# Two hand-ordered programs for the first two bodies of a pipelined attention, mixture-of-experts and cross-attention kernel

## The chip, the cores and the metric

The kernel runs on one core of one Trainium2 chip. A core has TensorE for matrix products (PE in the profile), VectorE (DVE), ScalarE (ACT), GpSimd (POOL) and SyncE (SP), which here only issues DMAs. Each engine runs its own list of instructions in order, and engines wait for each other on semaphores. The metric is the device time of one execution in microseconds, the median over the runs.

## The reference, cut to what matters

x has 2 batches of 1024 tokens of width 256; the context has 64 keys of width 192 for each batch. Four sublayers follow one another, each on the layer norm of the running x:

```python
x = x + L0_xattn(layernorm(x), ctx)   # 16 heads of 16, then relu(out @ W1 + b1) @ W2 + b2 (width 512)
x = x + L0_ffn(layernorm(x))          # 1024-wide FFN, 8 experts of LoRA rank 16, top 2, gate = top-2 softmax sum
x = x + L1_xattn(layernorm(x), ctx)   # one head of width 256
x = x + L1_ffn(layernorm(x))          # x @ weight.T + pooled(x) @ disha
```

## The kernel before, in words

**Tiling.** The 2048 tokens are cut into 8 blocks of T = 256 (two tiles of 128). A block goes through three stages: A is the first sublayer, F the expert layer, C the last two sublayers. They are pipelined: `body(a, f, c, h)` does stage A of block a, F of block f = a - 1, C of block c = a - 2, and the norm and queries (the head of stage A) of block h = a + 1. Body 0 so has no F and no C part, and body 1 no C part. After body 7 come `drain` and `end`.

**Precision.** Most products run in three passes: a value is split into a high part, rounded to the fp32r type by ScalarE, and a low part, the difference, made by VectorE or GpSimd; the passes are high by high, low by high, high by low (`passes` L306, `three` L296). So each operand needs two elementwise steps before its last pass. Products of type F32 (constants, transposes, fillers, `a_attend`) leave two records each in the profile.

**Stage A.** `transposes(1, b)` (L322) turns the normed block; `a_queries` (L334) makes the queries in bank P_(0); ScalarE's `queries` (L798) and VectorE's `queries_low` (L1060) split them; SyncE's `stack_q` (L227) lays them out head by head in the tensor `stack` with 12 DMAs for a block, 8 that wait for the high part and 4 for the low part. `a_row_scores` (L345) and `row_max` give each query's maximum, which `a_max_transposes` and ScalarE's `maxima` (L804) put into `stack` too. Then come `a_scores` d = 0 to 3 (L367) into banks S_(0) and S_(1) in turn, ScalarE's `exps` (L811) behind each, `a_attend` m = 0, 1 (L383) into P_(0) and P_(1), VectorE's `attended` (L1071: a reciprocal and a product), the split of the result, `a_hidden` u = 0, 1 (L397, with W1), `a_out` (L408, with W2) and the residual with the statistics of the second norm.

**Stage F.** `f_gate` (L420), VectorE's `experts` (L1084: the top two and the masked LoRA rows), `f_lora_transposes` (L431), `lora_high` and `lora_low` (L1122); then for u = 0 to 3 `f_base` (L437, weights wi), `f_first` and `f_second` (both through L458), and `f_out` (L474, weights wo), all in banks I_(0) and I_(1). Stage C begins with `c_turn` (L490) at the end of the body before, ScalarE's `high(3, ...)`, VectorE's `low(3, ...)` and `c_scores` (L503).

**Work of the first bodies alone.** The weights are loaded once by SyncE and ScalarE and split by `high_weights` (ScalarE L880) and `low_weights` (VectorE L1351, GpSimd L1518). `constant_row`, `keys1`, `values1`, `folded_keys` (L570 to L603) and the three `fold_` functions (L528 to L553) fold the weights and the context of stage C together. `filler` (L618) multiplies zeros into a bank that nothing reads: 3 of them stand ahead of body 0 and 10 in it.

**What sets the order.** Every engine has the order written out by hand. All bodies share one function for each engine, with branches for the stages that a body has and for a == 0 and f == 0. SyncE's order is fixed too: all weights and the stacks of block 0, then for each block `stack_q(b, 0)`, `stack_q(b, 2)`, `stack_q(b, 1)` and the load of the next x.

Of the kernel before, what the change touches and what calls it, by code (L numbers as in the profile page):

```python
# [11 lines left out]
P = 128  # L12
# [6 lines left out]
T = 256  # L19
# [40 lines left out]
def build(nc, io):  # L60
# [135 lines left out]
    bvrow1, wq1t = (views(passing, PASSING)[n] for n, _ in PASSING)  # L196
    kt0_h, kt0_l = temp("kt0_h", [P, KC * P], F32R), temp("kt0_l", [P, KC * P], F32R)
    kd_h, kd_l = temp("kd_h", [P, BATCH * KC * P], F32R), temp("kd_l", [P, BATCH * KC * P], F32R)
    kt1 = temp("kt1", [P, KC * P])
# [18 lines left out]
    with block:  # L218
# [74 lines left out]
        def _(pe):  # L293
# [40 lines left out]
            def a_queries(b):  # L334
                if b == 0:
                    pe.wait_ge(S("lo_w"), 1)
                else:
                    pe.wait_ge(S("o32"), (b - 1) * KC + 1)
                parts = [(P_(0)[:, m * T:(m + 1) * T], w("wq", m * P), x_of(XTA)) for m in range(KC)]
                pe.wait_ge(S("ln1_h"), b + 1)  # L340
                passes(parts, range(KC), ((0, 0), (1, 0)), True, False)
                pe.wait_ge(S("ln1_l"), b + 1)
                passes(parts, range(KC), ((0, 1),), False, True).then_inc(S("q_ps"), 1)

            def a_row_scores(b, t, bank=S_):  # L345

                if t == 0:
# [35 lines left out]
            def a_attend(b, m):  # L383
# [5 lines left out]
                for d in (2 * m, 2 * m + 1):  # L389
                    pe.wait_ge(S("ex"), b * DPAIRS + d + 1)  # L390
                    for c in (2 * d, 2 * d + 1):
                        rows = slice(PW * (c % GPC), PW * (c % GPC) + PW)
                        mm(P_(m)[rows, 0:T], v0[:, at + c * PW:at + (c + 1) * PW], EX[:, c, :], start=True, stop=True)  # L393
                        last = mm(P_(m)[rows, T:2 * T], ones_pair, EX[:, c, :], start=True, stop=True)  # L394
                last.then_inc(S("pv"), 1)

            def a_hidden(b, u):  # L397
                if u == 0:
                    if b == 0:
                        pe.wait_ge(S("lo_w"), 2)  # L400
                    pe.wait_ge(S("oh"), (b + 1) * KC)
                parts = [(S_(u)[:, k * T:(k + 1) * T], w("w1", (2 * u + k) * P), x_of(OA)) for k in range(2)]
                passes(parts, range(KC), ((0, 0), (1, 0)), True, False)
                if u == 0:
                    pe.wait_ge(S("ol"), (b + 1) * KC)
                passes(parts, range(KC), ((0, 1),), False, True).then_inc(S("hs_ps"), 1)
# [121 lines left out]
            def fold_turn():  # L528
                pe.wait_ge(S("g_in"), BATCH)
# [128 lines left out]

            def body(a, f, c, h):
                A_, F_, C_, H_ = (v is not None for v in (a, f, c, h))  # L660
                if A_:
                    a_scores(a, 0)
                    a_scores(a, 1)
                if F_:
                    f_lora_transposes(f)
                if C_:
                    c_scores(c, 0)
                    c_scores(c, 1)
                if F_:
                    f_first(f, 0)  # L670
                    f_first(f, 1)
                if A_:
                    a_scores(a, 2)
                if a == 0:
# [943 lines left out]
```

## Time and profile before

| | us |
|---|---|
| median of 3 runs | 330.58 |
| lowest, highest | 329.61, 331.83 |
| the profiled execution, whole | 332.24 |
| its span, first to last instruction | 330.1 |
| mean granted TensorE clock in the span | 0.988 of full |

The trace is of the profiled execution, and its times count from the start of the span. A busy share is of the span. A matmul's record begins when it starts and ends at a modelled end, so records of neighbours overlap; the chain of waits gives each step only the time by which it moved the chain on. Body 0 begins with `a_scores(0, 0)`, body 1 at 52.25 us and body 2 at 89.41 us.

### The profile page before, as it was taken

What the parts mean: (1) busy time and instruction counts of PE and PEld (TensorE: products, weight loads), DVE (VectorE), ACT (ScalarE), POOL (GpSimd) and SP (SyncE); (2) the same over time, 40 slices, a digit from 0 to 9 for tenths busy, and PEclk for the clock granted to TensorE, in tenths of its full rate; (3) what the DMA queues carried; (4) which work ended last, traced back from release to release, by engine and by line L of the source; (5) the groups of instructions that cost most, each with busy time, mean ns of one, the idle gap of its engine ahead of it and who ended that gap; (6) DMA issues with size and microseconds to landing.
All of it is one profiled execution on the core that took longest, in us unless ns stands there. A gap on an engine that the chain in (4) does not pass through costs nothing.

```text
span 330.1 us, 6479 instructions
## 1 busy us (share of the span) xinstructions
PE 314.6 (95%) x2497; PEld 285.6 (87%) x2497; DVE 231.2 (70%) x644; ACT 173.7 (53%) x355; POOL 146.2 (44%) x150
## 2 busy tenths in 40 slices
PE   7989998999999999999999999999999999999982
PEld 5748897899988999899989997999899988999771
DVE  4746676747878667956886687677786669456766
ACT  3346746572585456564667267635854564534411
POOL 2563681636053723654173607280537234613341
PEclk9989999999999999999999999999999999999997
DMA  8589720003100230013000410032002200000000
GB/s 244 156 247 359 165 82 0 2 9 89 32 3 2 57 92 13 2 26 104 36 0 10 96 57 0 2 85 77 2 0 50 69 13 1 2 0 34 0 34 32
DMA packets 14702, 18.85 MB, mean 57 GB/s; under 512 B 2224, under 2 KB 11312, under 8 KB 14416
## 3 DMA queue, kind: packets, MB, share of 16 engines
q1 hardware_dynamic: 12640, 14.99, 16.9%
q10 hardware_dynamic: 2032, 3.44, 3.0%
q8 instruction: 20, 0.33, 0.4%
q14 instruction: 10, 0.08, 0.1%
HBM read 9.51 MB, written 2.62 MB: 37 GB/s over the span
## 4 chain that ended last, share of the span: by engine, by line
PE 76%; POOL 8%; ACT 5%; DVE 5%; DMA 2%; SPq 2%; issue 1%; DVEq 0%; POOLq 0%; ACTq 0%
PE psI L302 13%; PE psI L458 12%; PE psI L311 9%; PE psP L311 7%; PE psS L311 7%; PE psT L302 4%; POOL hid_l L1447 4%; PE psP L393 3%; POOL hs_l L1441 3%; PE psS L379 2%; PE psT L326 2%; PE psP L394 2%; PE psT L525 2%; ACT qu_h L801 2%; PE psI L620 1%; ACT hs_h L829 1%
## 5 line engine op out<-in xcount | busy, mean ns | idle before, releaser
L1428 POOL TENSOR_TENSOR rs<-ve,mhalf 128x2 f32<-128x2 f32 x30 | 22.3, 745 | 95.3 <-DVE ve L1053 95.3
L1447 POOL TENSOR_TENSOR hid_l<-r,hid_h 128x512 fp32r<-128x512 f32 x32 | 40.8, 1288 | 15.3 <-ACT hid_h L849 15.3
L1132 DVE SCALAR_TENSOR_TENSOR r<-psI,nbi,r 128x256 f32<-128x256 f32 x60 | 25.8, 479 | 25.3 <-PE psI L458 25.2
L458 PE MATMUL psI<-at_h,lb_h 128*128 128x256 f32 x120 | 36.5, 304 | 2.1 <-DVE at_l L1124 1.5
L1441 POOL TENSOR_TENSOR hs_l<-hs,hs_h 128x512 fp32r<-128x512 f32 x16 | 20.8, 1301 | 35.6 <-ACT hs_h L829 35.4
L458 PE MATMUL psI<-at_l,lb_h 128*128 128x256 f32 x120 | 33.9, 282 | 0.0
L458 PE MATMUL psI<-at_h,lb_l 128*128 128x256 f32 x120 | 33.8, 282 | 0.0
L1073 DVE RECIPROCAL rec<-psP 128x256 f32<-128x256 f32 x16 | 28.1, 1753 | 6.5 <-PE psP L394 6.5
L844 ACT ACTIVATE r<-psI,first 128x256 f32<-128x256 f32 x60 | 24.2, 469 | 13.6 <-PE psI L458 13.5
L458 PEld LDWEIGHTS psI<-at_h,lb_h 128*128 128x128 f32 x120 | 22.6, 188 | 8.7 <-issue 5.0
L813 ACT ACTIVATE ex<-psS 128x512 f32<-128x512 f32 x32 | 19.0, 596 | 20.2 <-PE psS L379 20.1
L791 ACT ACTIVATE xn<-xmid,nmr,rs 128x256 f32<-128x256 f32 x16 | 8.8, 598 | 37.1 <-POOL nmr L1432 37.1
L302 PE MATMUL psI<-xtf_h,wi_h 128*128 128x256 f32 x120 | 25.3, 292 | 0.0
L302 PE MATMUL psI<-xtf_h,wi_l 128*128 128x256 f32 x120 | 24.0, 281 | 0.0
L302 PE MATMUL psI<-xtf_l,wi_h 128*128 128x256 f32 x120 | 24.0, 281 | 0.0
L849 ACT ACTIVATE hid_h<-r 128x512 fp32r<-128x512 f32 x32 | 19.5, 628 | 7.7 <-DVE r L1132 7.4
L458 PEld LDWEIGHTS psI<-at_h,lb_l 128*128 128x128 f32 x120 | 22.7, 189 | 0.2
L458 PEld LDWEIGHTS psI<-at_l,lb_h 128*128 128x128 f32 x120 | 22.6, 189 | 0.0
L1069 DVE TENSOR_REDUCE mx<-psS 128x16 f32<-128x1024 f32 x15 | 18.3, 1221 | 5.4 <-PE psS L356 5.4
L1436 POOL TENSOR_TENSOR oa_l<-o,oa_h 128x256 fp32r<-128x256 f32 x16 | 11.8, 737 | 18.7 <-ACT oa_h L818 18.7
L807 ACT ACTIVATE stack<-psP 16x1024 fp32r<-16x1024 f32 x16 | 16.2, 1016 | 7.0 <-PE psP L365 6.8
L302 PEld LDWEIGHTS psI<-xtf_h,wi_h 128*128 128x128 f32 x120 | 18.3, 189 | 0.7
(258 smaller groups left out, 870.6 us busy)
## 6 DMA issues: line engine op xcount, KB each, us to landing
stack<-qu_h SPq DMA_DIRECT2D x60, 64.0 KB, 2.0
xin<-in_x SPq DMA_DIRECT2D x8, 256.0 KB, 2.8
stack<-qu_l SPq DMA_DIRECT2D x30, 64.0 KB, 2.0
out<-x ACTq DMA_DIRECT2D x7, 256.0 KB, 2.0
raw_wi<-in_wi SPq DMA_DIRECT2D x1, 1024.0 KB, 9.1
raw_wo<-in_wo SPq DMA_DIRECT2D x1, 1024.0 KB, 12.4
kv<-in_kv SPq DMA_DIRECT2D x2, 384.0 KB, 8.4
raw_w<-in_w ACTq DMA_DIRECT2D x1, 512.0 KB, 7.5
```

Source lines behind the costliest of these rows:

```text
L302: last = mm(out, lhs(a, c), rhs(b, c), start=start and q == 0 and k == 0, stop=stop and q == 2 and k == n - 1, **kw)
L311: last = mm(out, lhs(a, c), rhs(b, c), start=start and (a, b) == pairs[0] and i == 0 and k == 0, stop=stop and k == len(chunks) - 1, skip_ ...
L458: last = mm(bank[:, k * T:(k + 1) * T], (WH, WL)[x]["lb"][:, 0, f * P:(f + 1) * P], AT[y][:, which, :], start=False, stop=q == 2, skip_gro ...
L813: A(EX[:, 2 * d:2 * d + 2, :], S_(d % 2).rearrange("p (k n) -> p k n", k=2), ACT.Exp, scale=SCALE).then_inc(S("ex"), 1)
L844: last = A(R1[:, f, :], bank[:, k * T:(k + 1) * T], ACT.Relu, bias=cols[:, BI + f:BI + f + 1])
L849: A(HH[:, 2 * u:2 * u + 2, :], R1[:, 2 * u:2 * u + 2, :], ACT.Identity).then_inc(S("hidh"), 1)
L1069: V.reduce_max(MX[:, t, :], ps[:, :].rearrange("p (h k) -> p h k", h=HEADS), AX.X).then_inc(S("mx"), 1)
L1073: V.reciprocal(REC[:, m, :], P_(m)[:, T:2 * T]).then_inc(S("rec"), 1)
L1132: last = V.scalar_tensor_tensor(out=R1[:, f, :], in0=bank[:, k * T:(k + 1) * T], scalar=nbi[:, f:f + 1], in1=R1[:, f, :], op0=MAX, op1=ADD)
L1428: G_.tensor_tensor(rs[:, :], ve[:, :], mhalf[:, :], ALU.pow).then_inc(S(f"ln{j}_rs"), 1)
L1441: G_.tensor_tensor(HS[1][:, two, :], HS32[:, two, :], as32(HS[0][:, two, :]), ALU.subtract).then_inc(S("hsl"), 1)
L1447: G_.tensor_tensor(HL[:, two, :], R1[:, two, :], as32(HH[:, two, :]), ALU.subtract).then_inc(S("hidl"), 1)
```

## The change

The first two bodies get functions of their own, `first_body` and `second_body`, on TensorE, ScalarE, VectorE and GpSimd; the shared `body` runs from body 2 on and loses its branches, its order being the same. SyncE's list is unchanged.

- Ahead of body 0 the fillers go from 3 to 5; in it they go from 10 to 4 (in T_(0)).
- In the first body all four `a_scores` of block 0 stand first, then both `a_attend`. `a_queries(1)` and `a_hidden(0, 0)` are cut into a high and a low part that alternate. `a_hidden(0, u)` writes the banks I_(u) of the feed-forward part, which leaves S_ free: the first `a_row_scores` of block 1 go to S_(0) and S_(1), the second to T_(0) and T_(1), without waits for the hidden layer or for the first maximum, and the transposed maxima to S_(0).
- All of block 1's `a_scores` and `a_attend` move from the second body into the first; `a_attend(1, 0)` writes T_(0). `f_lora_transposes(0)` moves ahead of them and of `f_base(0, 1)`. `values1` goes to T_(1) and moves behind `a_attend(1, 0)`.
- The fold work moves: `folded_keys` and `fold_turn` from the first body into the second, and `fold_means` and `fold_values` to its later half. Their helpers on ScalarE (`folded_in`, v1t, vv_h, gw_h) and on VectorE (`values_bias`, wc_sum, gw, gw_l, vv_l) move along. `gw_l` now stands between `experts(1)` and `low(3, 0)`; before, it stood ahead of `hidden_sum(0, 3)`.
- ScalarE converts `wi` directly ahead of `hidden(0, 0)`, as before; `w2` moves between the two halves of `attended`, and `queries(1)` between `hidden_high(0, 0)` and `hidden(0, 1)`.
- The buffer kt1 gets another place; `a_attend` takes a bank as an argument like `attended` below.

```diff
-    def a_queries(b):
-        if b == 0:
-            pe.wait_ge(S("lo_w"), 1)
-        else:
-            pe.wait_ge(S("o32"), (b - 1) * KC + 1)
+    def a_queries(b, high=True, low=True):
         parts = [(P_(0)[:, m * T:(m + 1) * T], w("wq", m * P), x_of(XTA)) for m in range(KC)]
-        pe.wait_ge(S("ln1_h"), b + 1)
-        passes(parts, range(KC), ((0, 0), (1, 0)), True, False)
-        pe.wait_ge(S("ln1_l"), b + 1)
-        passes(parts, range(KC), ((0, 1),), False, True).then_inc(S("q_ps"), 1)
+        if high:
+            if b == 0:
+                pe.wait_ge(S("lo_w"), 1)
+            else:
+                pe.wait_ge(S("o32"), (b - 1) * KC + 1)
+            pe.wait_ge(S("ln1_h"), b + 1)
+            passes(parts, range(KC), ((0, 0), (1, 0)), True, False)
+        if low:
+            pe.wait_ge(S("ln1_l"), b + 1)
+            passes(parts, range(KC), ((0, 1),), False, True).then_inc(S("q_ps"), 1)
...
-            if b > 0:
+            if b > 1:
                 pe.wait_ge(S("hs"), b * NDH)
-        elif b > 0:
+        elif b > 1:
             pe.wait_ge(S("mx"), b * NT + t)
...
-    def a_max_transposes(b):
+    def a_max_transposes(b, bank=P_(1)):
...
-        if b > 0:
+        if b > 1:
...
-        nc.tensor.transpose(P_(1)[0:NT * MXW, 0:P], mx[:, :], ident).then_inc(S("mxT_ps"), 1)
+        nc.tensor.transpose(bank[0:NT * MXW, 0:P], mx[:, :], ident).then_inc(S("mxT_ps"), 1)
...
-    def a_hidden(b, u):
-        if u == 0:
-            if b == 0:
-                pe.wait_ge(S("lo_w"), 2)
...
+    def a_hidden(b, u, banks=S_, high=True, low=True):
+        parts = [(banks(u)[:, k * T:(k + 1) * T], w("w1", (2 * u + k) * P), x_of(OA)) for k in range(2)]
+        if high:
+            if u == 0:
+                if b == 0:
+                    pe.wait_ge(S("lo_w"), 2)
+                pe.wait_ge(S("oh"), (b + 1) * KC)
+            passes(parts, range(KC), ((0, 0), (1, 0)), True, False)
+        if low:
+            if u == 0:
+                pe.wait_ge(S("ol"), (b + 1) * KC)
+            passes(parts, range(KC), ((0, 1),), False, True).then_inc(S("hs_ps"), 1)
...
     def fold_turn():
-        pe.wait_ge(S("g_in"), BATCH)
         pe.wait_ge(S("v1"), 1)
...
     def values1():
         for b in range(BATCH):
-            last = values(I_(1)[:, b * D:(b + 1) * D], kv1[:, WV1:WV1 + 2 * D], b)
+            last = values(T_(1)[:, b * D:(b + 1) * D], kv1[:, WV1:WV1 + 2 * D], b)
         last.then_inc(S("v1_ps"), 1)
...
     def folded_keys():
         pe.wait_ge(S("kt1"), 1)
-        pe.wait_ge(S("crow"), 1)
         pe.wait_ge(S("ld_passing"), 32)
...
-        last.then_inc(S("g_ps"), 1)
         for k in range(KC):
-            last = mm(I_(0)[:, 0:P], cols[:, BQ1 + k:BQ1 + k + 1].broadcast_to([P, P]),
+            last = mm(T_(0)[:, KC * P:(KC + 1) * P], cols[:, BQ1 + k:BQ1 + k + 1].broadcast_to([P, P]),
                       kt1[:, k * P:(k + 1) * P], start=k == 0, stop=k == 1)
         last.then_inc(S("gb_ps"), 1)
...
+    def first_body():
+        for d in range(DPAIRS):
+            a_scores(0, d)
+        a_attend(0, 0)
+        a_attend(0, 1)
+        pe.wait_ge(S("v0"), BATCH)
+        filler(T_(0), 2)
+        transposes(1, 1, T_(1))
+        filler(T_(0), 2)
+        a_queries(1, low=False)
+        a_hidden(0, 0, I_, low=False)
+        a_queries(1, high=False)
+        a_hidden(0, 0, I_, high=False)
+        a_hidden(0, 1, I_)
+        a_out(0, 0)
+        pe.wait_ge(S("ex"), DPAIRS)
+        a_row_scores(1, 0)
+        a_row_scores(1, 1, T_)
+        a_out(0, 1)
+        a_max_transposes(1, S_(0))
+        constant_row()
+        keys1()
+        transposes(2, 0, T_(1))
+        a_scores(1, 0)
+        a_scores(1, 1)
+        f_gate(0, 1)
+        a_scores(1, 2)
+        a_scores(1, 3)
+        pe.wait_ge(S("crow"), 1)
+        a_attend(1, 0, T_(0))
+        values1()
+        pe.wait_ge(S("kt1"), 1)
+        f_base(0, 0)
+        f_lora_transposes(0)
+        pe.wait_ge(S("x1"), 1)
+        a_attend(1, 1)
+        f_base(0, 1)
+
+    def second_body():
+        f_first(0, 0)
+        f_first(0, 1)
+        pe.wait_ge(S("o32"), KC + 1)
+        folded_keys()
+        f_second(0, 0)
+        f_second(0, 1)
+        a_hidden(1, 0)
+        pe.wait_ge(S("v1"), 1)
+        transposes(1, 2, T_(1))
+        f_base(0, 2)
+        a_hidden(1, 1)
+        f_first(0, 2)
+        f_base(0, 3)
+        a_queries(2)
+        f_second(0, 2)
+        f_first(0, 3)
+        a_out(1, 0)
+        a_row_scores(2, 0)
+        a_out(1, 1)
+        f_second(0, 3)
+        pe.wait_ge(S("g_in"), BATCH + 1)
+        fold_turn()
+        fold_means()
+        f_out(0, 0)
+        a_row_scores(2, 1)
+        f_out(0, 1, low=False)
+        fold_values()
+        pe.wait_ge(S("gw"), 1)
+        transposes(2, 1, T_(1))
+        f_out(0, 1, high=False)
+        a_max_transposes(2)
+        f_gate(1, 2)
+        pe.wait_ge(S("vv_l"), 2)
+        c_turn(0)
+        f_base(1, 0)
+        f_base(1, 1)
...
-    filler(I_(0), 3)
-    for i in range(NBLK):
-        body(i, i - 1 if i >= 1 else None, i - 2 if i >= 2 else None, i + 1 if i + 1 < NBLK else None)
+    filler(I_(0), 5)
+    first_body()
+    second_body()
+    for i in range(2, NBLK):
+        body(i, i - 1, i - 2, i + 1 if i + 1 < NBLK else None)
     drain(NBLK - 1, NBLK - 2)
     end(NBLK - 1)
...
+    def folded_in():
+        act.wait_ge(S("gb_ps"), 1)
+        for b in range(BATCH):
+            A(GWR[:, :, b * (KEYS + D):b * (KEYS + D) + KEYS],
+              T_(0)[:, 0:KC * P].rearrange("p (c b k) -> p c b k", c=KC, b=BATCH)[:, :, b, :],
+              ACT.Identity).then_inc(S("g_in"), 1)
+        A(gb[:, :], T_(0)[:, KC * P:(KC + 1) * P], ACT.Identity).then_inc(S("g_in"), 1)
...

+    def first_body():
+        for d in range(DPAIRS):
+            exps(0, d)
+        normalise(1, 1, XIN)
+        high(1, 1, XTA, T_(1))
+        attended(0, 0)
+        high_weights("w2")
+        attended(0, 1)
+        high_weights("wi")
+        hidden(0, 0, I_)
+        hidden_high(0, 0)
+        queries(1)
+        hidden(0, 1, I_)
+        hidden_high(0, 1)
+        high_weights("ga")
+        high_weights("lb")
+        maxima(1, S_(0))
+        high_weights("wo")
+        normalise(2, 0, XMID)
+        high(2, 0, XTF, T_(1))
+        for d in range(DPAIRS):
+            exps(1, d)
+        sorted_exps(0)
+
+    def second_body():
+        lora_high(0)
+        act.wait_ge(S("v1"), 1)
+        A(VV[0][:, 0:2 * BATCH:2, :], r3(v1, BATCH), ACT.Identity).then_inc(S("vv_h"), 1)
+        first_relu(0, 0)
+        attended(1, 0)
+        first_relu(0, 1)
+        folded_in()
+        attended(1, 1)
+        normalise(1, 2, XIN)
+        sum_high(0, 0)
+        hidden(1, 0)
+        hidden_high(1, 0)
+        high(1, 2, XTA, T_(1))
+        sum_high(0, 1)
+        first_relu(0, 2)
+        hidden(1, 1)
+        queries(2)
+        hidden_high(1, 1)
+        first_relu(0, 3)
+        act.wait_ge(S("v1t_ps"), 1)
+        A(v1t[:, :], T_(0), ACT.Identity).then_inc(S("v1t"), 1)
+        sum_high(0, 2)
+        sum_high(0, 3)
+        act.wait_ge(S("gw"), 1)
+        A(gw_h[:, :], gw[:, :], ACT.Identity).then_inc(S("gw_h"), 1)
+        normalise(2, 1, XMID)
+        act.wait_ge(S("vw_ps"), 1)
+        A(VV[0][:, 1:2 * BATCH:2, :], T_(0).rearrange("p (b n) -> p b n", b=BATCH), ACT.Identity).then_inc(
+            S("vv_h"), 1)
+        high(2, 1, XTF, T_(1))
+        maxima(2)
+        high(3, 0, XTC, T_(0))
...
-    def attended(b, m):
+    def attended(b, m, bank=None):
+        bank = P_(m) if bank is None else bank
         dve.wait_ge(S("pv"), b * KC + m + 1)
-        V.reciprocal(REC[:, m, :], P_(m)[:, T:2 * T]).then_inc(S("rec"), 1)
+        V.reciprocal(REC[:, m, :], bank[:, T:2 * T]).then_inc(S("rec"), 1)
         dve.wait_ge(S("rec"), b * KC + m + 1)
-        V.tensor_tensor(O32[:, m, :], P_(m)[:, 0:T], REC[:, m, :], MULT).then_inc(S("o32"), 1)
+        V.tensor_tensor(O32[:, m, :], bank[:, 0:T], REC[:, m, :], MULT).then_inc(S("o32"), 1)
...
+    def first_body():
+        dve.wait_ge(S("x_in"), 2 * 16)
+        norm_stats(1, 1, XIN)
+        attended(0, 0)
+        attended(0, 1)
+        low(1, 1, XTA, T_(1))
+        low_weights("wi", 1, 2)
+        queries_low(1)
+        row_max(1, 0)
+        row_max(1, 1, psT)
+        first_residual(0)
+        dve.wait_ge(S("x1"), 1)
+        norm_stats(2, 0, XMID)
+        low_weights("ga")
+        low_weights("lb")
+        constant()
+        low(2, 0, XTF, T_(1))
+        experts(0)
+        gates(0)
+
+    def second_body():
+        values_bias()
+        lora_low(0)
+        attended(1, 0, T_(0))
+        attended(1, 1)
+        dve.wait_ge(S("x_in"), 3 * 16)
+        norm_stats(1, 2, XIN)
+        hidden_sum(0, 0)
+        hidden_sum(0, 1)
+        dve.wait_ge(S("vv_h"), 1)
+        V.tensor_tensor(VV[1][:, 0:2 * BATCH:2, :], r3(v1, BATCH), as32(VV[0][:, 0:2 * BATCH:2, :]),
+                        SUB).then_inc(S("vv_l"), 1)
+        low(1, 2, XTA, T_(1))
+        dve.wait_ge(S("ld_wc"), 16)
+        V.tensor_tensor(GWR[:, :, KEYS:KEYS + D], GWR[:, :, KEYS:KEYS + D],
+                        late[:, D:2 * D].unsqueeze(1).broadcast_to([P, KC, D]), ADD).then_inc(S("wc_sum"), 1)
+        hidden_sum(0, 2)
+        queries_low(2)
+        row_max(2, 0)
+        hidden_sum(0, 3)
+        first_residual(1)
+        dve.wait_ge(S("x1"), 2)
+        norm_stats(2, 1, XMID)
+        dve.wait_ge(S("gw_mean"), 1)
+        V.tensor_tensor(GWR, GWR, T_(1)[:, 0:GW].unsqueeze(1).broadcast_to([P, KC, GW]), SUB).then_inc(
+            S("gw"), 1)
+        row_max(2, 1)
+        low(2, 1, XTF, T_(1))
+        dve.wait_ge(S("vv_h"), 2)
+        V.tensor_tensor(VV[1][:, 1:2 * BATCH:2, :], T_(0).rearrange("p (b n) -> p b n", b=BATCH),
+                        as32(VV[0][:, 1:2 * BATCH:2, :]), SUB).then_inc(S("vv_l"), 1)
+        second_residual(0)
+        dve.wait_ge(S("x2"), NT)
+        statistics(3, 0, X2)
+        experts(1)
+        dve.wait_ge(S("gw_h"), 1)
+        V.tensor_tensor(gw_l[:, :], gw[:, :], as32(gw_h[:, :]), SUB).then_inc(S("gw_l"), 1)
+        low(3, 0, XTC, T_(0))
+        moments(3, 0)
...
+
+    def values_bias():
         dve.wait_ge(S("ld_passing"), 32)
         dve.wait_ge(S("v1_ps"), 1)
-        V.tensor_tensor(r3(v1, BATCH), I_(1).rearrange("p (b n) -> p b n", b=BATCH),
+        V.tensor_tensor(r3(v1, BATCH), T_(1).rearrange("p (b n) -> p b n", b=BATCH),
                         bvrow1.unsqueeze(1).broadcast_to([P, BATCH, D]), ADD).then_inc(S("v1"), 1)
...
+    def first_body():
+        scale(1, 1)
+        attended_low(0, 0)
+        attended_low(0, 1)
+        low_weights("w2", 0, 1)
+        hidden_low(0, 0)
+        hidden_low(0, 1)
+        low_weights("wi", 0, 2)
+        scale(2, 0)
+        residual(1)
+        pool.wait_ge(S("crow_ps"), 1)
+        low_weights("wo", 0, 2)
+        low_weights("wo", 1, 2)
+
+    def second_body():
+        pool.wait_ge(S("crow"), 1)
+        gated(0)
+        attended_low(1, 0)
+        attended_low(1, 1)
+        scale(1, 2)
+        sum_low(0, 0)
+        sum_low(0, 1)
+        hidden_low(1, 0)
+        hidden_low(1, 1)
+        sum_low(0, 2)
+        sum_low(0, 3)
+        scale(2, 1)
+        residual(2)
+        scale(3, 0)
+
```

## Rows read from the trace of the kernel before

**Rows 1.** The page: span, TensorE's busy share, its granted clock in 40 slices.
```profile
span 330.1 us, 6479 instructions
PE 314.6 (95%) x2497; PEld 285.6 (87%) x2497; DVE 231.2 (70%) x644; ACT 173.7 (53%) x355; POOL 146.2 (44%) x150
PEclk9989999999999999999999999999999999999997
```

**Rows 2.** Waits of TensorE: for whom, us in total, times, longest.
```profile
PE psI L458 <- DVE at_l L1124: 1.5, 1, 1.5
...
PE psS L379 <- DMA stack<-qu_l: 1.2, 1, 1.2
```

**Rows 3.** The chain of waits from 0 to 110 us: start, us, what.
```profile
22.62 1.03 PE psP L393 x8
...
28.89 2.16 PE psI L620 x10
31.05 2.85 PE psS L311 x24
...
39.85 3.45 PE psT L574 x16
43.30 0.89 PE psI L582 x8
44.20 1.73 PE psI L567 x8
...
46.36 0.89 PE psT L597 x8
...
52.88 0.45 PE psP L434 x4
...
54.83 1.67 PE psI L458 x12
...
56.73 0.59 PE psP L393 x8
...
90.48 1.76 PE psT L302 x12
```

**Rows 4.** Stretches of half a us: length, busy by engine, granted clock, DMA.
```profile
18.50:19.00 0.50, 0.01 (x1) 0.00 (x0) 0.39 (x1) 0.39 (x1) 0.50 (x1) 1.00 0.49 103
...
22.00:22.50 0.50, 0.50 (x2) 0.00 (x0) 0.00 (x0) 0.00 (x0) 0.46 (x1) 0.50 1.31 436
```

**Rows 5.** Timeline from 15 to 50 us, all engines: start, us, what.
```profile
20.23 0.42 SPq L246 DMA_DIRECT2D raw_wi<-in_wi  x1
...
24.60 1.76 DVE L1073 RECIPROCAL rec<-psP 128x256 f32<-128x256 f32 x1 [2.65 <-PE psP L394]
...
31.02 1.91 ACT L882 ACTIVATE wi_h<-raw_wi 128x2048 fp32r<-128x2048 f32 x1
...
35.38 0.84 ACT L801 ACTIVATE qu_h<-psP,first 128x256 fp32r<-128x256 f32 x2 [0.33 <-PE psP L311]
...
36.11 0.63 ACT L829 ACTIVATE hs_h<-hs 128x512 fp32r<-128x512 f32 x1
36.24 6.04 SPq L233 DMA_DIRECT2D stack<-qu_h  x8
...
36.82 1.29 POOL L1441 TENSOR_TENSOR hs_l<-hs,hs_h 128x512 fp32r<-128x512 f32 x1 [0.98 <-ACT hs_h L829]
...
42.33 2.57 SPq L233 DMA_DIRECT2D stack<-qu_l  x4
```

**Rows 6.** DMA issues: what, queue, how many, KB each, median us to landing.
```profile
stack<-qu_l SPq DMA_DIRECT2D x30, 64.0 KB, 2.0
...
raw_wi<-in_wi SPq DMA_DIRECT2D x1, 1024.0 KB, 9.1
```

**Rows 7.** Timeline of VectorE from 61 to 92 us.
```profile
70.24 0.95 DVE L1310 TENSOR_TENSOR gw_l<-gw,gw_h 128x768 fp32r<-128x768 f32 x1
...
89.39 0.69 DVE L1057 TENSOR_TENSOR xtc_l<-psT,xtc_h 128x512 fp32r<-128x512 f32 x1
```

More of the change, by code:

```diff
@@ L381, in a_scores, with a_attend @@
                 last.then_inc(S("sc"), 1)
-            def a_attend(b, m):
+            def a_attend(b, m, bank=None):
+                bank = P_(m) if bank is None else bank
                 if m == 0 and b % BPB == 0:
@@ new lines, in body @@
+            def body(a, f, c, h):
+                a_scores(a, 0)
+                a_scores(a, 1)
+                f_lora_transposes(f)
+                c_scores(c, 0)
+                c_scores(c, 1)
+                f_first(f, 0)
+                f_first(f, 1)
+                a_scores(a, 2)
+                a_attend(a, 0)
+                f_second(f, 0)
+                c_transpose(c)
+                f_second(f, 1)
+                a_scores(a, 3)
+                f_base(f, 2)
+                c_attend(c)
+                a_attend(a, 1)
+                f_first(f, 2)
+                f_base(f, 3)
+                f_second(f, 2)
+                f_first(f, 3)
+                a_hidden(a, 0)
+                if h is not None:
+                    pe.wait_ge(S("z"), (c + 1) * NT)
+                    transposes(1, h, T_(1))
+                a_hidden(a, 1)
+                if h is not None:
+                    a_queries(h)
+                f_second(f, 3)
+                a_out(a, 0)
+                if h is not None:
+                    a_row_scores(h, 0)
+                a_out(a, 1)
+                f_out(f, 0)
+                if h is not None:
+                    a_row_scores(h, 1)
+                f_out(f, 1, low=False)
+                transposes(2, a, T_(1))
+                f_out(f, 1, high=False)
+                if h is not None:
+                    a_max_transposes(h)
+                f_gate(a, h)
+                c_turn(f)
+                f_base(a, 0)
+                f_base(a, 1)
@@ new lines, in body @@
+            def body(a, f, c, h):
+                exps(a, 0)
+                lora_high(f)
+                exps(a, 1)
+                linear(c)
+                weights_exp(c)
+                first_relu(f, 0)
+                first_relu(f, 1)
+                exps(a, 2)
+                weights_high(c)
+                sum_high(f, 0)
+                exps(a, 3)
+                if h is not None:
+                    normalise(1, h, XIN)
+                sum_high(f, 1)
+                attended(a, 0)
+                first_relu(f, 2)
+                attended(a, 1)
+                first_relu(f, 3)
+                if h is not None:
+                    high(1, h, XTA, T_(1))
+                hidden(a, 0)
+                hidden_high(a, 0)
+                hidden(a, 1)
+                if h is not None:
+                    queries(h)
+                hidden_high(a, 1)
+                sum_high(f, 2)
+                sum_high(f, 3)
+                normalise(2, a, XMID)
+                high(2, a, XTF, T_(1))
+                if h is not None:
+                    maxima(h)
+                high(3, f, XTC, T_(0))
+                sorted_exps(a)
+                store(c)
@@ L1024, in _ @@
             maxima(0)
-            for i in range(NBLK):
-                body(i, i - 1 if i >= 1 else None, i - 2 if i >= 2 else None, i + 1 if i + 1 < NBLK else None)
+            first_body()
+            second_body()
+            for i in range(2, NBLK):
+                body(i, i - 1, i - 2, i + 1 if i + 1 < NBLK else None)
             drain(NBLK - 1, NBLK - 2)
@@ L1351, in low_weights @@
+                dve.wait_ge(S("x2"), (f + 1) * NT)
+                statistics(3, f, X2)
+                experts(a)
+                low(3, f, XTC, T_(0))
+                moments(3, f)
+                gates(a)
             def low_weights(n, k=0, parts=1):
@@ L1413, in _ @@
             dve.wait_ge(S("nbi"), 1)
-            for i in range(NBLK):
-                body(i, i - 1 if i >= 1 else None, i - 2 if i >= 2 else None, i + 1 if i + 1 < NBLK else None)
+            first_body()
+            second_body()
+            for i in range(2, NBLK):
+                body(i, i - 1, i - 2, i + 1 if i + 1 < NBLK else None)
             drain(NBLK - 1, NBLK - 2)
```

348 lines of the change are left out of this document (52 added, 296 removed).

## The prediction, made before the change was run

> **What bounds the kernel now.** I read the page first. TensorE is busy for 95% of the span [rows 1], VectorE for 70%: a change can gain only where TensorE has idle time, works at the lower clock or does work that isn't needed. The waits of TensorE come next: the longest are 1.5 us for `at_l` and 1.2 us for the stack's DMA [rows 2], and both lie in the first two bodies. Then the chain of waits: after the stretch of `a_scores` and exps it is TensorE's own work nearly throughout, but part of that work is filler. The last five fillers of body 0 take 2.16 us as ten records [rows 3], so 0.43 us for one; the ten in the body take some 4.9 us together, some of them at half clock. `a_hidden(0, 0)` starts at 31.05, as those fillers end [rows 3]. Last the clock: the granted clock is 1.00 at 18.5 us, where TensorE has run dry, and 0.50 at 22.0 [rows 4], that is 1.2 in place of 2.4 GHz. The same group of eight `a_attend` records takes 1.03 us there and 0.59 us in body 1 [rows 3]. Stretches of half a microsecond read one after the other show 0.50 or nearly so from 21.6 to 25.0 us, which gives up half of 3.4 us, 1.7 us of work. So of the time up to body 2 about 4.9 us are filler, 1.7 us are clock and some 3.5 us are waits: 10 us that a better order could reach for.
>
> The Trainium skill (TensorE: Matmul & The Clock Gate, Why this matters for your kernels) tells one to leave no idle gaps between bursts of matmuls, because they bring the clock down. The trace agrees: 1.2 us and then 0.5 us of idle time, with 0.5 us of work between them, stand ahead of the fall [rows 4]. This speaks against the change where it opens gaps; the price below is from rows.
>
> **Step 1, to the queries of block 1.** The two more fillers ahead of body 0 take 0.86 us in a gap of 1.2 us that ends with the stack's landing at 19.3, so they cost nothing. All four `a_scores` with their exps are over at about 22.6 (ScalarE takes 0.6 us for each and starts at 20.2). Both `a_attend` end by 23.7, or 25.4 at half clock. VectorE's chain of two reciprocals of 1.76 us [rows 5] and two products of 0.42 us then gives the second attended half at 27.2 to 28.2, before at 29.2. TensorE finishes both `a_hidden` and the queries of block 1 at 31 to 32, where before it only began. That lead of up to 4 us is not kept, by ScalarE's order: it must convert `wi` before it can take `hidden(0, 0)`, and `wi` is issued at 20.23 [rows 5] and lands 9.1 us later [rows 6], at 29.35. The conversion takes 1.91 us and started at 31.02 before [rows 5]; it can now start 1.7 us earlier and end at 31.3. Then hidden 0.84, its high part 0.63 and the queries 0.84 us [rows 5] give the queries of block 1 at 33.6; before they ended at 36.2. TensorE waits some 1.7 us for the first high part. The lead here is 2.6 us, whatever the clock was at 22 us.
>
> **Step 2, the stack of block 1.** SyncE is untouched: 12 DMAs, 6.04 and 2.57 us of issue [rows 5], and the last lands 2.0 us after its issue [rows 6]. From 33.65 that is 44.3. Between lie `hidden(0, 1)` and its high part (1.5 us), GpSimd's low part of 1.29 us [rows 5] and the last `a_out` (0.95 us): x1 is ready at 37.4, against 39.4. `constant_row` and `keys1` take 3.45 and 0.89 us [rows 3], to 41.8; the transposes of the second norm then wait for ScalarE, which has `maxima` (2.05 us) and the conversion of `wo` (1.9 us) ahead of `normalise(2, 0)`, and end at 43.0. Now `a_scores(1, 0)` stands in TensorE's list ahead of `f_gate` and waits for the stack until 44.3. Before, the stack landed at 46.9 and TensorE came to it at 52.2, so this wait was hidden; moving the scores ahead uncovers it. TensorE is idle for about 2.0 of the 2.5 us from 41.8 to 44.3.
>
> **Step 3, from 44.3 to the first LoRA product.** Before, the chain from 46.36 to the end of the LoRA transposes at 53.33 is 6.97 us [rows 3]. Taken out of it: `folded_keys` (0.89 [rows 3] and 0.45 for its second half), the transposed maxima and `fold_turn`, together 1.9 us. Put in: two more `a_scores` 0.48, two `a_attend` of 1.02 each (two groups as in rows 3 that overlap a little), `values1` 1.73 [rows 3], together 4.25 us. That is 9.3 us, all dense, since the experts on VectorE (2.9 us behind the gate) and the split of the LoRA rows (0.61 and 0.70 us) now lie beside them; the 1.5 us wait for `at_l` [rows 2] goes. `f_first(0, 0)` starts at 53.6, before at 54.83 [rows 3]: 1.2 us early, with 0.7 us less work left (2.5 us of scores and attends done already, 1.8 us of fold work added).
>
> **Step 4, the second body.** In the kernel before, 37.4 us pass from 54.83 to the end of `c_scores(0)` at 92.24 [rows 3]. Less the 0.7 us: 36.7. What is late next are three new waits. (a) VectorE starts `attended(1, 0)` only after `lora_low`, at 52.5; two of them (4.45 us), the statistics of block 2 (1.3), GpSimd's power (1.0) and ScalarE's normalise (1.1) make the transposes of block 2 ready at 60.4, and TensorE is there at 59.2: 1.1 us. (b) `f_out(0, 0)` waits for the last high part of the hidden sum, which on ScalarE now stands behind v1t and so behind `fold_turn`: 0.6 us. (c) `gw_l`, 0.95 us [rows 7], now stands between `experts(1)` and `low(3, 0)`. Before, that low part started at 89.39 and `c_scores` at 90.48 [rows 7, 3], with only some 0.4 us to spare. I take 0.8 us for this. None of these three waits is in the trace of before: each can be 0, if TensorE comes 1 us later than I reckon, and together they may be twice the 2.5 us. 53.6 and 36.7 and 2.5 give 92.8 for the end of `c_scores(0)`, against 92.24: 0.6 us later. Behind it the order is the old one, so the difference stays to the end.
>
> **The clock.** The gap at 41.8 to 44.3 is like the one that preceded the fall at 21.6 (2.0 us idle of 2.5, then 1.7 of 2.2). If the clock falls, it does so in the dense stretch of step 3, where half of 3.4 us, 1.7 us, is lost on the path. At 22 us the lower clock costs the new kernel nothing (step 1). Bounds are 0 and 1.7 us; both look about as likely, I take 0.85.
>
> **Sum.** -1.2 (start of step 4) - 0.7 (work) + 2.5 (waits) + 0.85 (clock) = +1.4 us. The profiled execution took 332.24 us, 2.1 of it outside the span; it would become 333.7. It lies 1.7 us above the median, so the forecast for the median is 330.58 + 1.4 = 332.0 us: about no change. A difference of 1%, 3.3 us, is about what a measurement of this kernel can tell.
>
> **Rivals.** *TensorE stays dense (faster).* Only work counts, and my waits are hidden or short: six fewer fillers in body 0 save 2.6 us, the `at_l` wait 1.5, the early clock 1.7, with step 2's wait cut to 1 us: 5.8 - 1 = 4.8 us, 325.8 us. For it speaks that TensorE is the bound over the span [rows 1]. Against it: `wi` lands at 29.35 whatever the order, and 12 stack DMAs take 8.6 us to issue. *The stack lands late (slower).* SyncE's first eight issues took 6.04 us because the weights were still in flight until about 39.5. If the stack gets through only behind them and lands as late as before, at 46.9, TensorE waits 2.6 us more, all of it on the path, and the clock falls for certain: 0.6 + 2.6 + 1.7 = 4.9 us, 335.5 us. It decides from a landing after 46. *The waits of step 4 double (slower).* That is +2.5 on 1.4, 334.5 us; GpSimd's operations in the chain of (a) are the likeliest place.
>
> **How the numbers follow.** The forecast (small losses and gains that cancel) has 0.62, TensorE dense 0.18, the stack late 0.10, doubled waits 0.10. The dense case is faster by over 1% in most of its range; the two slow cases are beyond 1% (333.9) about as often as not, and the forecast's own spread of 2 us adds some. Faster 0.17, same 0.65, slower 0.18. The range takes in most of the dense case and nearly all of the late stack: 326.8 to 335.2.
>
> **What would show it.** Right: `wi_h` starting near 29.4 and `hidden(0, 0)` on ScalarE directly behind it; queries of block 1 near 33.6; a wait of TensorE for the stack's DMA of 1 to 2 us near 43 to 45; no wait for `at_l` in body 1; `f_first(0, 0)` near 53.6; a wait before the transposes of block 2; `c_scores(0)` over near 92.8, and the same pace from there. A clock of 0.50 for some 3.4 us within 44 to 50 would show the clock term. Wrong: `c_scores(0)` over before 90 (the dense case), or the stack landing after 46.

## The result, and the profile after

The changed kernel took 335.11 us in the median of four runs (332.51 to 335.65), against 330.41 for the kernel before, also in four: 4.7 us more. The ratio on record is 1.0101, with a 95% interval of 1.0064 to 1.0137. It is not the quotient of the two medians, which is 1.0142; with four runs a side both are rough. The forecast was 332.0 us and no change that can be told. The change is a small loss, clear of the interval; the time is past the 333.9 us from which the prediction called it slower, and lies within the range by 0.1 us only.

The page of the changed kernel shows TensorE busy for the same share as in [rows 1]. Its clock has moved: the dip that stood in the third slice now stands, deeper, in the sixth.

```profile
span 333.5 us, 6463 instructions
...
PE 316.6 (95%) x2489; PEld 286.6 (86%) x2489; DVE 232.4 (70%) x644; ACT 173.0 (52%) x355; POOL 147.0 (44%) x150
...
PEclk9999969999999999999999999999999999999998
```

The waits of TensorE from 15 to 96 us (for whom, us in total, times, longest):

```profile
PE psS L381 <- DMA stack<-qu_l: 1.4, 1, 1.4
PE psT L326 <- ACT xn L817: 1.0, 2, 0.8
PE psI L311 <- ACT oa_h L844: 0.7, 1, 0.7
PE psT L302 <- DVE xtc_l L1102: 0.6, 1, 0.6
PE psT L501 <- DVE x L1186: 0.6, 1, 0.6
PE psI L311 <- ACT hid_h L875: 0.5, 1, 0.5
```

The 1.5 us for `at_l` of [rows 2] are gone. In their place stand the stack's DMA, now in front of body 1's scores, and the three waits of step 4: for xn (0.8 us, the longer of its two; the other 0.2 us lies in body 0), for hid_h and for xtc_l.

Three stretches of the same trace (length, busy by engine, granted clock, DMA) show the price of the first of them:

```profile
42.00:43.00 1.00, 0.00 (x0) 0.00 (x0) 0.46 (x1) 0.51 (x1) 1.00 (x1) 1.00 0.80 148
43.00:43.50 0.50, 0.19 (x1) 0.22 (x2) 0.23 (x1) 0.00 (x0) 0.50 (x2) 1.00 0.61 230
44.50:50.50 6.00, 6.00 (x33) 4.28 (x33) 3.14 (x19) 1.59 (x4) 1.88 (x2) 0.50 0.00 0
```

TensorE is empty at 42 to 43 us. From 44.2 to 50.9 us the clock is 0.50, with matmul records over all of it: 33 matmuls in 6 us. In the same window two later runs whose clock held have 52 (the first) and 59 (the fifth); the one is 0.9 us behind the changed kernel there and the other 1.6 us ahead of it, so these are not quite the same matmuls. The chain of waits of the changed kernel, where it answers to the milestones of [rows 3]:

```profile
39.29 3.93 DMA stack<-qu_l
...
43.31 0.70 PE psS L381 x4
...
47.23 1.03 PE psT L396 x8
...
49.12 2.84 PE psT L571 x8
...
53.37 0.45 PE psP L439 x4
...
91.90 0.87 DVE gw_l L1369
92.77 0.61 DVE xtc_l L1102
...
93.52 2.00 PE psT L302 x12
```

The last stack DMA takes 3.93 us from issue to landing. The first eight `a_attend` records take 1.03 us and `values1` 2.84, for 0.59 and 1.73 in [rows 3]. `f_first(0, 0)` starts at 56.29, as the timeline has it:

```profile
56.29 0.28 PE L463 MATMUL psI<-at_h,lb_h 128*128 128x256 f32 x1
```

`gw_l` stands directly ahead of the low part that `c_scores(0)` waits for. `c_scores(0)` ends at 95.52, before at 92.24: 3.3 us later, and the whole span is 3.4 us longer. All of the loss was made by 95.5 us; TensorE's waits behind it are the same.

### The profile page after: what moved, and what is told of

Same layout as the page of the kernel before. It is cut to its first block, busy times and chain, and to the rows that moved or that the text cites. A ratio compares the mean times of both kernels' runs of the same rounds, so it can differ in the third digit from the quotient of the medians.

```text
span 333.5 us, 6463 instructions
## 1 busy us (share of the span) xinstructions
PE 316.6 (95%) x2489; PEld 286.6 (86%) x2489; DVE 232.4 (70%) x644; ACT 173.0 (52%) x355; POOL 147.0 (44%) x150
## 4 chain that ended last, share of the span: by engine, by line
PE 68%; DVE 10%; POOL 9%; ACT 7%; DMA 2%; SPq 2%; issue 2%; DVEq 0%; POOLq 0%; ACTq 0%
PE psI L302 12%; PE psI L463 11%; PE psI L311 9%; PE psP L311 7%; PE psS L311 5%; POOL hid_l L1513 5%; PE psT L302 4%; PE psS L381 2%; POOL hs_l L1507 2%; PE psP L396 2%; DVE rec L1119 2%; SPq L233 2%; PE psT L326 2%; PE psT L530 2%; POOL rs L1494 2%; ACT qu_h L827 2%
## 5 line engine op out<-in xcount | busy, mean ns | idle before, releaser
L1119 DVE RECIPROCAL rec<-psP 128x256 f32<-128x256 f32 x15 | 26.3, 1753 | 4.5 <-PE psP L397 4.5
L1114 DVE TENSOR_REDUCE mx<-psS 128x16 f32<-128x1024 f32 x14 | 17.1, 1222 | 6.8 <-PE psS L358 6.8
L302 PEld LDWEIGHTS psI<-xtf_h,wi_l 128*128 128x128 f32 x120 | 18.5, 189 | 0.0
```

The costliest lines, as they stand in the source:

```text
L302: last = mm(out, lhs(a, c), rhs(b, c), start=start and q == 0 and k == 0, stop=stop and q == 2 and k == n - 1, **kw)
L1114: V.reduce_max(MX[:, t, :], ps[:, :].rearrange("p (h k) -> p h k", h=HEADS), AX.X).then_inc(S("mx"), 1)
L1119: V.reciprocal(REC[:, m, :], bank[:, T:2 * T]).then_inc(S("rec"), 1)
```

## The experiments

Each run is compared with executions of the kernel before on the same chip: one chip for the first to the eighth, another for the ninth to the eleventh. The 82 executions of the kernel before fall into two groups by mean granted clock: 62 had 0.991 or more and a median of 330.5 us, 20 had 0.988 or less and 332.2. The mean clock does not sort them fully: seven of the 62 took 331.9 to 332.2 us too. The profiled one of the rows, at 0.988 and 332.24 us, is of the smaller group. The changed kernel had 0.989 or less in three of its four executions (334.6 to 335.7) and 0.993 in one (332.5).

**1. Fillers over the gap.**

```diff
                 keys1()
+                pe.wait_ge(S("ql"), 2 * KC)
+                filler(P_(0), 1)
                 transposes(2, 0, T_(1))
+                filler(P_(0), 3)
                 a_scores(1, 0)
```

> The changed kernel with four more fillers in the first body, one ahead of the transposes of the second norm and three behind them, in P_(0), to bridge the gap that ends with the stack's landing at 43.3 us. Theory (the clock): the 6.8 us at a granted clock of 0.50 behind that gap cost half of that, 3.4 us, all on TensorE's path. With the gap bridged the clock stays at 1.00, f_first(0, 0) starts near 52.7 instead of 56.2, and the median falls from 335.1 to about 331.8. Rival (the waits of the second body are what is lost): the fillers add nothing and take nothing away, the median stays within 0.5 of 335.1, even if the clock is better. Second rival (the lower clock only fills time that TensorE would wait anyway): clock 1.00 but c_scores(0) still ends near 95.5.

Measured: 334.12 us (332.08 to 339.63), ratio 1.0111 (1.0074 to 1.0148). Four of six executions had a clock of 0.990 or more, with a median of 333.2. In the profile the clock is whole from 44.5 to 50.5:

```profile
44.50:50.50 6.00, 6.00 (x52) 5.12 (x52) 3.96 (x20) 2.27 (x5) 2.83 (x3) 1.00 0.01 3
```

and `c_scores(0)` ends at 93.3 instead of 95.5. The stretch from the first scores of block 1 to `f_first(0, 0)` fell from 12.98 us (43.31 to 56.29) to 9.83 (44.25 to 54.08), so the clock was worth 3.1 us there, near the 3.4 expected. But the scores began 0.9 us later in this profile, since the queries of block 1 came 1.1 us later; and in the median only 1.0 us came through, as the clock did not hold in all executions and something else varied.

**2. The gate ahead of block 1's scores.**

```diff
-                a_scores(1, 0)
-                a_scores(1, 1)
                 f_gate(0, 1)
+                a_scores(1, 0)
+                a_scores(1, 1)
+                values1()
                 a_scores(1, 2)
                 a_scores(1, 3)
                 pe.wait_ge(S("crow"), 1)
                 a_attend(1, 0, T_(0))
-                values1()
```

> The changed kernel with f_gate(0, 1) ahead of a_scores(1, 0), and values1 between the second and the third of block 1's scores: the wait for the stack gets work in front of it, without fillers. Theory (the clock and the gap): the wait of 1.4 us for the stack's DMA goes, the gap shrinks to the split of the second norm (about 1 us), the clock stays at 1.00; 3.4 us for the clock and about 0.8 us for the gate moved into the gap, so about 331 us. Rival (the waits of the second body): at most 0.8 us, 334.3 us.

Measured: 335.69 us, ratio 1.0134 (1.0105 to 1.0163): no gain, both theories missed. TensorE still waited 2.5 us for the stack, though it came to it later. The tile view of `stack` gives the reason, the time from issue to landing (min, median, max) of block 1's stack DMAs, here for this run:

```profile
DMA to landing us min/median/max: 4.9/7.2/10.1
```

For the changed kernel the same line reads:

```profile
DMA to landing us min/median/max: 2.7/4.6/7.4
```

and for the kernel before:

```profile
DMA to landing us min/median/max: 2.0/2.5/3.3
```

All 12 were issued by 39.9 us in the changed kernel and by 40.5 in this run, but the last landed at 43.2 in the one and at 47.2 in the other. This is the point that the theory had missed. The loads ahead in the same queue show where the difference arises. SyncE issued `wc` at 25.01 in the profile of the changed kernel and at 27.60 in this one, and it landed 13.9 and 14.0 us later. In the five profiles with this order on SyncE (the changed kernel and the first four runs) the last stack DMA lands the later, the later `wc` does: 43.2, 44.2, 45.1, 46.0 and 47.2 us behind 38.9, 40.1, 40.4, 40.7 and 41.6.

**3. The three waits of the second body taken out.** One stretch for each of xn (VectorE, GpSimd, ScalarE), hid_h and xtc_l.

```diff
                 gates(0)
+                dve.wait_ge(S("x_in"), 3 * 16)
+                norm_stats(1, 2, XIN)
...
                 attended(1, 1)
-                dve.wait_ge(S("x_in"), 3 * 16)
-                norm_stats(1, 2, XIN)
...
                 gated(0)
+                scale(1, 2)
                 attended_low(1, 0)
                 attended_low(1, 1)
-                scale(1, 2)
...
+                normalise(1, 2, XIN)
                 first_relu(0, 0)
...
                 attended(1, 1)
-                normalise(1, 2, XIN)
...
+                sum_high(0, 2)
+                sum_high(0, 3)
                 act.wait_ge(S("v1t_ps"), 1)
                 A(v1t[:, :], T_(0), ACT.Identity).then_inc(S("v1t"), 1)
-                sum_high(0, 2)
-                sum_high(0, 3)
...
                 row_max(2, 1)
+                dve.wait_ge(S("gw_h"), 1)
+                V.tensor_tensor(gw_l[:, :], gw[:, :], as32(gw_h[:, :]), SUB).then_inc(S("gw_l"), 1)
                 low(2, 1, XTF, T_(1))
...
                 experts(1)
-                dve.wait_ge(S("gw_h"), 1)
-                V.tensor_tensor(gw_l[:, :], gw[:, :], as32(gw_h[:, :]), SUB).then_inc(S("gw_l"), 1)
                 low(3, 0, XTC, T_(0))
```

> The changed kernel with only the three waits of its second body taken out: the statistics, the power and the normalise of block 2 stand earlier on VectorE, GpSimd and ScalarE; the last two high parts of the hidden sum stand ahead of v1t on ScalarE; gw_l stands behind row_max(2, 1) instead of between experts(1) and low(3, 0). The gap in the first body stays. Theory (the clock is most of the loss): the three waits were 1.0, 0.5 and 0.6 us and gw_l 0.9 us of VectorE's path, so 2 us at most are won, about 333.2 us, and 0.50 still stands behind the gap. Rival (the waits are the loss): 330.5 us or below.

Measured: 335.01 us (330.42 to 335.58), ratio 1.0092 (1.0045 to 1.0140), next to nothing. Its profile was taken with a stack later still, for which TensorE stood 3.8 us:

```profile
PE psS L381 <- DMA stack<-qu_l: 3.8, 1, 3.8
```

The median is inconclusive on the waits: the stack varied by more than they are worth. The trace is not: from `f_first(0, 0)` to the end of `c_scores(0)` it has 36.5 us, where the changed kernel has 39.2.

**4. Both.** The edits of 2 and 3 together; on TensorE again

```diff
+                f_gate(0, 1)
                 a_scores(1, 0)
                 a_scores(1, 1)
-                f_gate(0, 1)
+                values1()
...
```

> e2 and e3 together: the gate ahead of the scores of block 1, and the three waits of the second body taken out. If both causes stand and add up: 335.1 - 4.2 - 2.0 = 329 us, below the kernel before. If the clock is the whole cause, the same as e2, about 331. If neither is, it stays near 335.

Measured: 331.90 us (328.99 to 333.72), ratio 1.0030 (0.9996 to 1.0064). Four executions at clocks from 0.993 had a median of 329.3, eight from 0.983 to 0.989 one of 333.2. What is left goes with the clock. Alone, the two edits had moved the median by +0.6 and -0.1 us, together by -3.2; no run shows why they do not add up.

**5. The stack ahead of the late loads.** On SyncE alone:

```diff
-            sp.dma_start(GWR[:, :, KEYS:KEYS + D], io["wc"].rearrange("p (c n) -> p c n", c=KC)).then_inc(S("ld_wc"), 16)
-            sp.wait_ge(S("kd_out0"), 32)
-            keys_in(0, 0, 1)
-            keys_in(0, 1, 1)
-            sp.wait_ge(S("kd_out1"), 32)
-            keys_in(1, 2, 1)
             for b in range(1, NBLK):
...
                 stack_q(b, 1)
+                if b == 1:
+                    sp.dma_start(GWR[:, :, KEYS:KEYS + D], io["wc"].rearrange("p (c n) -> p c n", c=KC)).then_inc(S("ld_wc"), 16)
+                    sp.wait_ge(S("kd_out0"), 32)
+                    keys_in(0, 0, 1)
+                    keys_in(0, 1, 1)
+                    sp.wait_ge(S("kd_out1"), 32)
+                    keys_in(1, 2, 1)
```

> The changed kernel with one thing moved on SyncE: the loads that nothing needs before body 1 or body 4 (wc, and the three key blocks of batch 1, 0.6 MB) are issued behind the 12 stack DMAs of block 1 instead of ahead of them. Theory (the stack lands late because it queues behind the weights): in the profiles so far its last piece landed between 43.2 and 47.2 us though it was issued by 40.4 at the latest; now it lands by 42.5 in every execution, TensorE's wait for it is under 0.5 us, the clock falls less often, and the median goes from 335.1 to about 331.5, with less spread. Rival (the landing is not the traffic ahead of it): landing and median as in the changed kernel, 335. Rival (the waits of the second body are the loss): landing early, median still above 333.5.

Measured: 331.35 us (330.74 to 336.30), ratio 1.0032 (1.0008 to 1.0055), as the theory said: 335.11 - 331.35 = 3.8 us back between the medians by moving DMAs alone. The ratios on record differ by 0.7%, 2.3 us, and their intervals do not overlap. In the one execution that was traced the last stack DMA landed at 41.6; 11 of 12 executions had a mean clock of 0.990 or more, though one of these took 334.48 us. The line of the tile view of `stack`, and then the window behind the gap, now read:

```profile
DMA to landing us min/median/max: 2.0/2.5/4.3
```

```profile
44.50:50.50 6.00, 6.00 (x59) 4.41 (x58) 5.01 (x20) 2.22 (x5) 2.69 (x3) 1.00 0.11 31
```

**6. All three.** The edits of 2, 3 and 5 together, with nothing else; on SyncE again

```diff
                 stack_q(b, 1)
+                if b == 1:
...
```

> The last run of before (gate ahead of the scores of block 1, the three waits of the second body out, 331.9 us) with the same move on SyncE. If the late stack with the clock behind it and the three waits are the whole loss, no wait for the stack is left, the clock stays at 1.00 through body 1, and the median is 328 to 329 us, below the kernel before. If the landing doesn't matter: 331.9.

Measured: 330.08 us (328.61 to 333.21), ratio 0.9992 (0.9961 to 1.0023). Only 5 of 12 executions were above 0.989 in clock. The median was 329.2 for those and 331.2 for the rest: without a wait for the stack worth the name (0.3 us in the profile), the clock was still lower in seven of twelve.

**7 and 8. Controls on the kernel before.** The same move on SyncE, in the seventh, and two more fillers ahead of body 0 in the eighth:

```diff
-            filler(I_(0), 3)
+            filler(I_(0), 5)
```

> The kernel before with the same move on SyncE. Its TensorE comes to the first scores of block 1 only at 52 us, some 5 us behind the landing. Theory: nothing changes, 330.5 us within 0.5. If it gets faster, the late traffic costs the kernel before something too, and the last two runs must be read against this one.

> The kernel before with one part of the change alone: five fillers instead of three ahead of body 0. Theory: the clock no longer falls at 21.6 us, the work of body 0 up to a_hidden runs at full speed, but a_hidden(0, 0) then waits for the attended halves, so of the 1.7 us of clock 1 us at most comes through: 329.5 to 330.5 us. Rival (the lower clock there lies beside waits): 330.5, unchanged.

Measured: 330.56 us, ratio 1.0003 (0.9980 to 1.0027), and 330.64 us, ratio 0.9999 (0.9983 to 1.0014). Neither changes anything in the median. That was the theory of the seventh, and the rival of the eighth, whose theory had hoped for up to 1 us. With five fillers all 12 executions were at 0.992 or more and the highest took 331.70 us, but the median execution of the kernel before is so without them.

**9 to 11. What is left, piece by piece,** with the stack early as in 5 in all three. The ninth is the sixth with four fillers in the gaps; the tenth has the edits of 3 alone; the eleventh has the fillers alone:

```diff
                 a_hidden(0, 1, I_)
+                filler(P_(1), 2)
                 a_out(0, 0)
...
                 keys1()
+                pe.wait_ge(S("ql"), 2 * KC)
+                filler(P_(0), 1)
                 transposes(2, 0, T_(1))
+                filler(P_(0), 1)
```

> The best version so far (gate ahead of the scores of block 1, the three waits of the second body out, stack DMAs ahead of the late loads; 330.1 us with single executions from 328.6 to 333.2 and clocks from 0.984 to 0.996) with four fillers laid into what is left of TensorE's gaps in the first body: two ahead of a_out(0, 0), one on each side of the transposes of the second norm. Theory (what is left of the spread is the clock, which falls in some executions behind those gaps): the slow executions go, the median falls to about 329.0 us and the highest below 331. Rival (the fillers themselves lie on the path, or the spread is the landing of the weights): 330.1 or above, same spread.

> The changed kernel with the stack DMAs ahead of the late loads (331.35 us with that alone) and the three waits of the second body taken out, order of gate and scores as in the changed kernel. It prices the three waits by themselves now that the stack is early. Theory: they were 1.0, 0.5 and 0.6 us, so 331.35 - 2.0 = 329.3 us. Rival (they are only pushed to the next wait, as the run with the waits alone suggested, 335.0 against 335.1): 331 us. Rival: the gate's place, not the waits, made the last run good, then 331 us too.

> The changed kernel with the stack DMAs ahead of the late loads and the same four fillers. It prices the clock by itself with an early stack. Theory: the executions at 334 and above go and the median, already at 331.35 without a fall in most executions, comes to 331.0; the clock was the consequence of the late stack and not a cause of its own. Rival (the clock is a cause of its own): 329.5 us or below.

Measured, all three nearer to the theory than to the rivals (the eleventh 0.6 us above it):

```
                        median us   ratio to before (95% interval)   c_scores(0) ends
all and fillers         329.36      0.9949 (0.9925 to 0.9972)        89.3
stack and waits         329.02      0.9958 (0.9929 to 0.9988)        88.6
stack and fillers       331.58      1.0013 (0.9993 to 1.0033)        91.4
```

All 12 executions of both runs with fillers have a mean clock of 0.990 or more (highest 330.96 and 332.43 us), and the fillers move the median by little: from 330.08 to 329.36 us and from 331.35 to 331.58, each time on another chip. The three waits are worth 331.35 - 329.02 = 2.3 us, once the stack is early; this too is between chips, and the ratios, 1.0032 and 0.9958, give 2.4. The trace of the tenth run agrees: from the start of `f_first(0, 0)` to the end of `c_scores(0)` it has 36.6 us, against 39.2 in the changed kernel. Both ends of that stretch, of which the second was at 90.48 before and at 93.52 in the changed kernel:

```profile
51.98 0.28 PE L464 MATMUL psI<-at_h,lb_h 128*128 128x256 f32 x1
```

```profile
86.84 1.76 PE psT L303 x12
```

The first two beat the kernel before by 0.4 to 0.5% and the changed kernel by more, and do not differ by more than their intervals. The tenth does so without the gate's move, which therefore isn't needed.

## Why the prediction was right, and where it was not

The order of events was right, and the parts that went wrong partly cancelled. That the median still lies inside the range, by 0.1 us, is luck: the profile moved by 3.3 us to the end of `c_scores(0)`, where 0.6 and 0.85 for the clock had been forecast.

**Step 1** held. ScalarE waited for `wi` and converted it at 28.03 (forecast 29.35), `hidden(0, 0)` stood directly behind it, and the queries of block 1 were ready at 32.2 (33.6), since `wi` landed 1.3 us sooner than in the trace of before. TensorE waited 0.2 us for the first high part, not 1.7. The two fillers cost nothing. But I had counted the lower clock at 21.6 us among what a better order could reach. To go by the mean clock, the kernel before has it in 20 of 82 executions, and the eighth run shows that its removal moves the median by nothing.

**Step 2** had the right wait (1.4 us at 41.9 to 43.3) and the wrong time to landing. 2.0 us was the median over all 90 such DMAs of the trace, most of them issued when the weights had landed; behind the weights the last of the 12 took 3.9 us. Three things made up for that in the profile: the queries came 1.4 us earlier, the twelve issues began within 7.0 us instead of 8.1, and the sum had counted the last issue twice, 0.6 us, since the time to landing starts with the issue (so the stack before landed at 46.35, not 46.9). The scores began at 43.3, 1.0 us before the forecast. The 6.04 us of the first eight issues had been put down to weights in flight; here the same eight took 5.07, all of them with loads in flight, and before, a single issue of 1.57 us at 40.1 made the difference.

In the profiles of the second and third run, with the same order on SyncE, the scores began as late as 47.3 and 46.0. I had a landing after 46 as a rival, priced at 335.5 us with a chance of 0.10. The trace of the changed kernel does not show it; but the fifth run shows that the loads ahead of the stack make most of the loss, by the wait and by the clock behind it. SyncE issues all of them, and with the body-0 order of the change it decided by its own order which landed late: with `wc` and the keys ahead, the stack's DMAs took 2.7 to 10.1 us; with the stack ahead, 2.0 to 4.5. (In the kernel before, where the stack is issued later, they take 2.0 to 3.3 with `wc` and the keys ahead as well.) The Trainium skill (DMA: Bandwidth & Descriptors, Queues, rings and completion order) says that a DMA engine takes the descriptors of one issuer in the order of issue. These runs agree; weighed beforehand, it would have pointed at this price.

**Step 3** held: the stretch from the stack to `f_first(0, 0)` is 9.8 us at full clock (the first and the eleventh run; 9.3 reckoned), and the 1.5 us for `at_l` are gone.

**Step 4** held. The waits were expected at 1.1, 0.6 and 0.8 us and their sum at 2.5. In the trace they stand at 0.8, 0.5 and 0.6; what they cost together is the 39.2 us from `f_first(0, 0)` to the end of `c_scores(0)` less the 36.6 of the tenth run, 2.6 us, and 2.3 between the medians. The 36.7 us reckoned for that stretch without waits were right to 0.1.

**The clock** is the term that was mis-sized. I took 0.85 us, half of the 1.7 that 3.4 us at the lower level cost in the kernel before. Here the clock was lower in three of four executions, and in the traced one it stayed at 0.50 for 6.8 us, which is 3.4 us of work. In numbers of the profile: scores 1.0 us early, 3.4 us for the clock, 0.3 us more for the matmuls of step 3 and the second body as reckoned give 92.8 - 1.0 + 3.4 + 0.3 = 95.5, where `c_scores(0)` ended; the 92.8 had no clock in it.

**The base** was mis-sized too. I added the difference from a profiled execution that had paid for a fall of its own to a median execution that had not. Between the two profiles the change costs 3.4 us, between the medians 4.7.

So the new order did about what had been reckoned of it, and the loss was made in two places: at the stack of block 1 with the clock behind it (3.8 us between the medians) and in the second body (2.3 us). With both out, what the new order is worth shows: the tenth run is 0.4% (1.4 us) faster than the kernel before.

Not tried: which of the late loads, wc or the keys of batch 1, holds the stack; and why SyncE's issues of the weights, and with them the landing of `wc`, differ by up to 2.6 us between profiles. What makes the clock fall in one execution and not in another stays open as well.

## What to carry to other kernels

Moving a consumer (here the scores) ahead in one engine's list is only worth it if its operand's transfer can come sooner too: look at what else is in the DMA queues when it is issued, and take its time to landing from a row of that stretch, not from the median over the program. Loads that nothing needs for a while belong behind the transfer that the next stage waits for. When executions differ, read the granted clock of each before comparing two profiles: a gain or a loss of half a per cent can be one fall of the clock that only one of the two has.

## What was not expected of the hardware

The clock stayed at 0.50 for 6.8 us under TensorE records without a gap, twice as long as the 3.4 us before. `a_attend` and `values1` were among them, as was `a_attend` in the shorter case. The profiles of the second and third run also have 6.8 us at 0.50, that of the fourth 3.4.

Small SBUF-to-SBUF DMAs of 64 KB needed between 2.0 and 10.1 us from issue to landing. They were the same twelve each time; the kernels differ in what stood ahead of them in the queue and in when they were issued.
